# Scatters of 128 rows in place of 125 in the counting sort of a graph network kernel

## What is computed

```python
edge_index = jnp.stack([src, dst])
h = jnp.maximum(_layernorm(x, axis=-1), 0.0)
x = x + _L0_gnn_ref(h, src, dst, edge_type_8, ...)       # typed messages, sum, GRU
h = jnp.maximum(_layernorm(x, axis=-1), 0.0)
x = x + _L1_gnn_ref(h, edge_attr_16, ..., src, dst)      # attention with a segment maximum
h = jnp.maximum(_layernorm(x, axis=-1), 0.0)
x = x + _L2_gnn_ref(h, edge_index, edge_weight, ...)     # four graph convolutions
h = jnp.maximum(_layernorm(x, axis=-1), 0.0)
x = x + _L3_gnn_ref(h, edge_index, ...)                  # sheaf messages
```

## Time and profile before

| | us |
|---|---|
| median of 3 runs | 8238.34 |
| the runs | 8218.16 to 8241.7 |
| the profiled execution, its own time | 8244.08 |
| its span | 8242.4 |
| mean granted TensorE clock | 0.828 |
| POOL busy | 4496.5 (55% of the span) |
| DVE busy | 5955.1 (72%) |
| PE busy | 5734.8 (70%) |

### The profile page before, as it was taken

The page is one execution under the profiler, slowest core; times in us unless marked ns, Lnnn a source line. Parts: engine busy times, 40 slices in busy tenths (PEclk is TensorE's granted clock), DMA queues, the critical chain, the costliest instruction groups (busy, mean ns, idle before and its releaser), DMA issues. The chain is left out here.

```text
span 8242.4 us, 120531 instructions
## 1 busy us (share of the span) xinstructions
PE 5734.8 (70%) x33629; PEld 3891.4 (47%) x33630; DVE 5955.1 (72%) x11485; ACT 1609.0 (20%) x2672; POOL 4496.5 (55%) x4143
## 2 busy tenths in 40 slices
PE   3433333256444588887699999455479699999999
PEld 2333333146444455555455555144334366666555
DVE  5766555275333499998899999799600388888898
ACT  0010111101000255554122222044000022222000
POOL 0488888487777577777377777200000277777000
PEclk9999999855555699999899999699889655555899
DMA  2122222332111333334211111022263411112000
GB/s 99 41 60 57 56 55 58 77 83 53 37 37 36 49 84 85 83 85 79 42 44 43 44 43 44 15 109 110 80 264 136 151 32 32 32 32 32 1 0 1
DMA packets 486789, 514.88 MB, mean 62 GB/s; under 512 B 258365, under 2 KB 388805, under 8 KB 476106
## 3 DMA queue, kind: packets, MB, share of 16 engines
q1 hardware_dynamic: 343198, 446.64, 17.5%
q0 software_dynamic: 132160, 43.97, 6.7%
q10 hardware_dynamic: 11232, 21.73, 0.9%
HBM read 415.02 MB, written 95.99 MB: 62 GB/s over the span
## 5 line engine op out<-in xcount | busy, mean ns | idle before, releaser
L1284 POOL DMA_INDIRECT sh_ring<-node,sh_idx x832 | 858.6, 1032 | 1488.2 <-DVE sh_idx L1921 1229.4
L424 POOL DMA_INDIRECT slots<-rank_staged,rank_row_i x800 | 998.7, 1248 | 265.5 <-issue 260.0
L1533 POOL DMA_INDIRECT slots<-sm_rec,sm_row x832 | 900.0, 1082 | 388.0 <-issue 215.2
L1360 POOL DMA_INDIRECT mx_ring<-node,mx_idx x832 | 857.8, 1031 | 322.3 <-issue 248.5
L935 POOL DMA_INDIRECT mid_ring<-typed,mid_idx x832 | 875.8, 1053 | 259.2 <-issue 253.4
L404 PE MATMUL rank_found<-rank_next_sb,rank_hot_hi_t 25*125 25x128 f32 x1600 | 374.3, 422 | 764.0 <-ACT rank_next_sb L386 748.5
L1643 PE MATMUL sm_sums<-sm_both,sm_hot 128*128 128x512 f32 x1664 | 786.8, 595 | 0.4 <-DVE sm_both L1564 0.2
L404 PEld LDWEIGHTS rank_found<-rank_next_sb,rank_hot_hi_t 25*125 25x125 f32 x1600 | 347.4, 323 | 789.8 <-issue 734.9
L1140 PE MATMUL mid_sums<-mid_ring,mid_hot_d 128*128 128x17 f32 x1664 | 391.7, 375 | 459.3 <-DMA mid_ring<-typed,mid_idx 446.9
L1140 PEld LDWEIGHTS mid_sums<-mid_ring,mid_hot_d 128*128 128x128 f32 x1664 | 383.3, 312 | 476.0 <-issue 476.0
L2161 PE MATMUL srl_sums<-srl_outer,srl_hot_lo 128*128 128x400 f32 x1664 | 561.9, 501 | 7.4 <-DVE srl_outer L2143 7.4
(11 more groups left out here) (404 smaller groups left out, 12727.3 us busy)
## 6 DMA issues: line engine op xcount, KB each, us to landing
strips<-near SPq DMA_DIRECT2D x76, 1600.0 KB, 14.4
mx_far<-far_row SPq DMA_DIRECT2D x208, 256.0 KB
rank_key_row<-key_rows SPq DMA_DIRECT2D x100, 488.3 KB
near<-adj_whole SPq DMA_DIRECT2D x175, 256.0 KB, 2.0
sm_low<-low_row SPq DMA_DIRECT2D x208, 128.0 KB
sh_low<-low_row SPq DMA_DIRECT2D x104, 256.0 KB, 3.3
feat_t<-mid_out ACTq DMA_DIRECT2D x104, 204.0 KB
mx_feat<-feat_t SPq DMA_DIRECT2D x208, 102.0 KB
```

Of the source, the lines that this page charges most:

```text
L424: pool.indirect_dma_start(m.slots, bass.IndirectOffsetOnAxis(ap=row_i[:, h, j:j + 1], axis=0), staged[:, h, j, :], None).then_inc(sent[h], 16)
L1284: pool.indirect_dma_start(ring[:, h, j, :], None, table, bass.IndirectOffsetOnAxis(ap=idx[:, h, j:j + 1], axis=0)).then_inc(part, 16)
L1360: pool.indirect_dma_start(ring[:, n % DEEP, j, :], None, m.node40, bass.IndirectOffsetOnAxis(ap=idx[:, t:t + 1], axis=0)).then_inc(gathere ...
L1533: pool.indirect_dma_start(m.slots2, bass.IndirectOffsetOnAxis(ap=row2[:, t:t + 1], axis=0), rec2[:, t, :], None).then_inc(ordered, 16)
```

## The change

The row numbers and the staged records become tiles of 128 partitions, the DMAs of line 424 take them whole, and the table `slots` gets 2,048 rows more. Before the loop POOL writes row numbers past the table's end into all partitions and zeros into all staged records; DVE and ACT then overwrite only the first 125 partitions. So in each scatter three rows of zeros go to fixed rows past the table's end, different ones for each partition, half and group. DVE and ACT wait for these two instructions once, ahead of their loops. The readers of `slots` take the first SLOTS rows.

```diff
-            whole = m.slots.rearrange("(p c n) k -> p c (n k)", p=P, n=32)
+            whole = m.slots[0:SLOTS, :].rearrange("(p c n) k -> p c (n k)", p=P, n=32)
...
-        row_i = sb("row_i", [EP, 2, NS], I32)
-        staged = sb("staged", [EP, 2, NS, REC])
+        row_i = sb("row_i", [P, 2, NS], I32)
+        staged = sb("staged", [P, 2, NS, REC])
...
@@ vector
             for h in range(2):
                 dve.sem_inc(row_used[h], 1)
+            dve.wait_ge(primed, 2)
...
-                nc.vector.scalar_tensor_tensor(row_i[:, h], pos[:, 2, :], float(NT), pos[:, 1, :], ALU.mult,
+                nc.vector.scalar_tensor_tensor(row_i[0:EP, h], pos[:, 2, :], float(NT), pos[:, 1, :], ALU.mult,
                                                ALU.add).then_inc(at_row[h], 1)
@@ scalar
             act.wait_ge(seeded, 1)
+            act.wait_ge(primed, 2)
...
-                    nc.scalar.copy(staged[:, h], edges[:, :, bass.ds(s, 1), :].rearrange("p j o k -> p j (o k)")).then_inc(rec_in[h], 1)
+                    nc.scalar.copy(staged[0:EP, h], edges[:, :, bass.ds(s, 1), :].rearrange("p j o k -> p j (o k)")).then_inc(rec_in[h], 1)
@@ gpsimd
+            pool.iota(row_i[:, :, :], pattern=[[NS, 2], [1, NS]], base=SLOTS, channel_multiplier=2 * NS).then_inc(primed, 1)
+            pool.memset(staged[:, :, :, :], 0.0).then_inc(primed, 1)
             for h in range(2):
                 pool.dma_start(m.spare[h:h + 1, :], m.zero_row[0:1, 0:D]).then_inc(sent[h], 16)
@@ middle
-        slots = m.slots.rearrange("(q t) k -> q t k", q=P)
+        slots = m.slots[0:SLOTS, :].rearrange("(q t) k -> q t k", q=P)
@@ build
-    m.slots, m.spare = dram("slots", [SLOTS, REC]), dram("spare", [2, D])
+    m.slots, m.spare = dram("slots", [SLOTS + P * 2 * NS, REC]), dram("spare", [2, D])
```

More of the change, by code:

```diff
@@ L309, in rank_and_scatter @@
         state, at_row, rec_in, sent = pair("state"), pair("at_row"), pair("rec_in"), pair("sent")
-        chain, seeded, loads = sem("chain"), sem("seeded"), sem("loads")
+        chain, seeded, loads, primed = sem("chain"), sem("seeded"), sem("loads"), sem("primed")
         edges = m.edges[:, :].rearrange("p (j s k) -> p j s k", j=NS, k=REC)
```

## The result

The changed kernel takes 8137.7 us (median of 4 runs, 8130.6 to 8140.4), the kernel before on the same chip 8229.3 us: a ratio of 0.9888, 95% interval 0.9875 to 0.9901, so 92 us or 1.1% faster. The prediction was 8153 in a range of 8100 to 8215, from 85 us of gain. The profiled execution has a span of 8136.6 us, 106 us under that of before.

What follows compares the result with a forecast made beforehand. GpSimd's scatters bound the sort at 12.42 us a column; shortened, they leave the load loop as bound at 11.6. The stage then ends at 1452, not 1537.3: 85 us gained, 8153 us from the median, range 8100 to 8215.

Steps and rivals of the forecast that it cites:

- The bound: Sort stage: GpSimd's scatters bound it at 12.42 us a column; after the change the load loop does, at 11.6.
- The rival in which the loads do not hold: Sort stage: loads speed up greatly, GpSimd stays the bound; gain 132 to 222 us, time 8016 to 8106; chance 0.07.
- The scatter: Line 424: with 128 rows it takes 975 ns in place of a median of 1184, within bounds of 972 and 1212.
- That rival, at 0.12: Line 424: the scatter does not get shorter, 1184 to 1212 ns; time the same or up to 22 us more; chance 0.12.
- The sharing of engines: Load loop: scatters hold 0.6 us per engine and column, not 1.06; loads regain half of 0.33 us; period 11.6.
- my lower end of 11.15: Load loop: shortest period in us a column, 11.75 - 0.86 x 0.71, for a gain of 129 us.
- The small parts: Sort stage: three more rows cost nothing; IOTA and MEMSET, some 0.1 and 0.5 us, are covered by the first load.
- The signs that I listed: Profile after: line 424 near 975 ns, no packet over 1 KB, some 350 us of `hi_row` waits, line 340 every 11.6 us.
- The slower rival: Load loop: scatter data on all 16 engines delays loads; at three times the engine time 75 us slower, 8313; chance 0.08.
- my range of periods: Load loop: 11.15 to 12.1 us a column, for gains of 129 to 37 us and times of 8109 to 8201.

Runs made afterwards that it cites:

- kind B: Not a run: the three chips of the follow-up groups on which the kernel before took 9359, 9317 and 9115 us.
- kind A: Not a run: the chips on which the kernel before took 8228 us in a follow-up group and 8229 us for the result.

## Why the prediction was right

**The bound** was named correctly. That the early 20 columns ran at the pace of the loads, 0.15 us under GpSimd, told that of a faster scatter little more would be left than the distance between 12.42 and about 11.6. The rival in which the loads do not hold needed 10.2 to 11.1 us a column; no stretch of the stage has that. The forecast was that of GpSimd's 170 us half would be paid out, 85; measured are 174 us saved and 97 of it in the stage. (The 170 is 800 x 0.212, which goes with 972 ns; with the 975 that I took it is 167.)

**The scatter** was put at 975 ns and is 958. The bound of 972 from 8-byte rows held for 96-byte rows; between rows of 8 and of 96 bytes no difference shows (959 and 958 ns in the profile after), between 8 and 25 rows per engine it does. The rule that the number of engines is the largest divisor up to 16 stands in the Trainium skill (DMA: Bandwidth & Descriptors, "Why a DMA increments its semaphore by 16 and not by 1"). By that rule the trace agrees, at 128 rows with 16 large packets and at 127 with a price of 2542 ns. The remark of the same page that more descriptors cost the generator little does not help here: 125 rows are three fewer in all, but 17 more on each engine that takes part, and they cost 226 ns more in every instruction. That rival, at 0.12, was wrong.

**The sharing of engines** was the one term chosen between far ends, and here the sum was right partly by luck. I took 0.6 us of engine time a column after the change; it is 0.046 x 11.47 = 0.53. I counted 0.15 us of what the loads could get back at most, 0.33, and put the period at 11.6. In the stretch from which the 11.75 came, the loop really gained 0.42 us, from 11.75 to 11.33. By the trace 0.28 us of that is the load (from the issue of `key_row` to the start of `hot_hi_t` 8.54 us before and 8.26 after, means of 21 and 22 columns) and 0.13 us is VectorE's own part up to the next issue (3.19 and 3.06 us), for which the sum had nothing. Against this stands an error the other way: I took the early stretch for the whole stage. The loop is slower in some stretches than in others, in the run with one scatter too (11.26 us in 290 to 545, 11.51 in 1115 to 1410), so over the stage it is 11.47. The two errors leave 0.13 us a column, the 12 us by which the stage ended earlier than the 1452 I gave: 1438.9 + 1.0 = 1439.9. The run with one scatter gives the floor, 11.37; my lower end of 11.15 could not be reached.

**The small parts** cost nothing that shows: with the width undone the time is that of the kernel before to some 15 us, and the first `hot_hi_t` of the changed kernel starts at 282.0, as before. The signs that I listed came: 800 scatters in 824.5 us, packets of 768 bytes and 9.87 MB, waits for `hi_row` of 351.8 us, line 341 every 11.3 to 11.6 us to the end, and loads that take 8.4 us from issue to use, none over 9.

**What the sum left out**: the profiled span fell by 106 us, 97 in the stage, 2 at its end and the rest behind it, mostly in the stage that follows, where nothing was changed. The medians fell by 92 and 100 us in two groups. I had put these stages at zero. Runs of the kernel before spread by 23 us, so no effect on them is shown.

**The slower rival** priced contention on the loads' engines. The loads never showed it; they got shorter. On the one chip of kind B where the changed kernel ran, 24 us were left of the gain, with TensorE's completions held up in the stage, and no rival of mine had that. A gain of 24 us lies outside the 37 to 129 us of my range of periods, so that the measurement fell on kind A was luck as well.

## What to carry to other kernels

Give indirect DMAs a number of rows with a large divisor up to 16: pad 125 to 128 with harmless rows, and avoid primes; the price of a scatter here went by the rows on one engine, from 936 ns at 7 to 2542 at 127. Before crediting a faster instruction with its whole saving, look for a stretch of the same stage in which another loop set the pace: its period is near what the stage will keep. It is not exact. The stretch may be a fast or a slow one, and the loop may itself speed up with the change, as it did here. And compare on more than one chip when GpSimd's back-to-back DMAs run beside TensorE: the same change brought 92 and 100 us on one kind of chip and 24 us, in one execution, on the other.

## What I had not expected of the hardware

The same kernel took 8228 us on one chip and 9115 to 9359 on three others. On these three, waits on TensorE in the sort's stage were released up to 20 us after its matmuls are shown as ended. They stood while GpSimd issued 128-row indirect DMAs without a pause, and most of the long ones ended only when it had none left to issue; with 125-row scatters in the same loop there was no such wait. Nearly all of the difference between two of the chips, 1041 of 1105 us, lies in the four stages with 128-row gathers or scatters. A scatter of 127 rows lengthened not only its own instruction but the gap before the next, from 0.30 to 0.77 us.
